# Waiting for the banks of two score tiles in front of the first of them

## What is computed

```python
q = (x @ Wq + bq).reshape(B, N, 16, 16)
k = (y @ Wk + bk).reshape(B, M, 16, 16)
v = (y @ Wv + bv).reshape(B, M, 16, 16)
scores = jnp.einsum('bnhd,bmhd->bhnm', q, k) * scale
attn = jax.nn.softmax(scores, axis=-1)
out = jnp.einsum('bhnm,bmhd->bnhd', attn, v).reshape(B, N, 256)
x = x + jnp.tanh(g_xattn[0]) * (jax.nn.relu(out @ W1 + b1) @ W2 + b2)
# then x + tanh(g_ffn[0]) * (shared expert + the top 2 of 8 routed experts)
```

## Time and profile before

| | us |
|---|---|
| median of three runs | 1035.18 |
| lowest and highest | 1034.99, 1036.46 |
| the profiled execution's own time | 1034.86 |
| its span from the first to the last instruction | 1033.1 |
| PE busy | 1011.9 (98%) |
| DVE busy | 680.7 (66%) |
| ACT busy | 612.1 (59%) |

### The profile page before, as it was taken

One profiled execution on the slowest core, in us unless ns is written; L12 is line 12 of the kernel. 1 busy time (PEld: TensorE's weight loads), 2 busy tenths in 40 slices (PEclk: granted clock), 3 DMA queues, 4 the chain that ended last, 5 costly groups with the idle time before them and its releaser, 6 DMA issues. The chain is left out here.

```text
span 1033.1 us, 15853 instructions
## 1 busy us (share of the span) xinstructions
PE 1011.9 (98%) x5821; PEld 559.6 (54%) x5821; DVE 680.7 (66%) x929; ACT 612.1 (59%) x1144; POOL 227.8 (22%) x225
## 2 busy tenths in 40 slices
PE   8899999999999999999999999998999999999998
PEld 5434445434445434544544453333666888888865
DVE  4999886896787798588788768712487322222227
ACT  3167777886677777577787767774375222222211
POOL 6129300105400103610010031020002333333310
PEclk9999999999999999999999999999999999999999
DMA  9263030430302403203033030011591111111107
GB/s 220 72 169 63 2 64 4 125 64 2 64 14 52 107 22 64 55 10 65 1 64 65 1 64 1 18 66 41 175 336 30 39 51 53 53 51 52 48 26 244
DMA packets 38282, 70.17 MB, mean 68 GB/s; under 512 B 6848, under 2 KB 23360, under 8 KB 38208
## 3 DMA queue, kind: packets, MB, share of 16 engines
q1 hardware_dynamic: 33072, 57.88, 21.6%
q0 software_dynamic: 3744, 10.23, 3.2%
q10 hardware_dynamic: 1392, 1.05, 0.4%
HBM read 33.70 MB, written 9.31 MB: 42 GB/s over the span
## 5 line engine op out<-in xcount | busy, mean ns | idle before, releaser
L770 ACT ACTIVATE probs<-ring_ps 128x512 f32<-128x512 f32 x816 | 434.0, 598 | 125.8 <-PE ring_ps L944 118.8
L1079 DVE TENSOR_REDUCE mpart<-gu_ps 128x2 f32<-128x1024 f32 x384 | 456.4, 1220 | 71.3 <-PE gu_ps L929 71.2
L944 PE MATMUL ring_ps<-qst,kst 64*128 64x512 f32 x816 | 221.8, 459 | 3.0 <-ACT probs L770 2.1
L959 PE MATMUL pv_ps<-probs,vp 128*32 128x512 f32 (+2 forms) x1664 | 222.7, 604 | 0.6 <-ACT osb L701 0.6
L944 PEld LDWEIGHTS ring_ps<-qst,kst 64*128 64x128 f32 x816 | 97.3, 180 | 205.4 <-ACT probs L770 116.2
L929 PE MATMUL gu_ps<-kst,qst 63*128 63x512 f32 (+1 forms) x1024 | 179.7, 396 | 8.7 <-DVE mpart L1079 7.5
L929 PEld LDWEIGHTS gu_ps<-kst,qst 63*128 63x128 f32 x1024 | 91.7, 185 | 64.1 <-DVE mpart L1079 40.3
L1309 ACT ACTIVATE h_sb<-gu_ps 128x512 f32<-128x512 f32 x55 | 32.8, 596 | 133.6 <-PE gu_ps L1463 133.6
L1516 DVE TENSOR_TENSOR h_sb<-h_sb,gu_ps 128x512 f32<-128x512 f32 x55 | 37.7, 686 | 112.6 <-ACT h_sb L1309 112.1
L1483 PE MATMUL y_ps<-wd,hT 128*128 x312 | 73.8, 379 | 0.0
L1300 POOL DMA_INDIRECT picked<-ysb,target x39 | 38.5, 988 | 131.5 <-DVE ysb L1557 131.5
(11 more groups left out here) (240 smaller groups left out, 1251.8 us busy)
## 6 DMA issues: line engine op xcount, KB each, us to landing
kst<-parts SPq DMA_DIRECT2D x45, 401.0 KB, 5.3
qst<-parts SPq DMA_DIRECT2D x48, 128.0 KB, 4.5
wgu<-in_WgT SPq DMA_DIRECT2D x16, 256.0 KB, 8.2
wgu<-in_WuT SPq DMA_DIRECT2D x16, 256.0 KB, 8.3
wd<-in_WdT SPq DMA_DIRECT2D x8, 512.0 KB, 9.8
wgu<-picked SPq DMA_DIRECT2D x8, 512.0 KB, 7.4
cold<-in_ctxT SPq DMA_DIRECT2D x3, 800.5 KB, 4.2
cold<-in_ctxT SPq DMA_DIRECT2D x6, 400.2 KB, 5.9
```

The source lines that it names most:

```text
L770: nc.scalar.activation(probs[0:w, m % NPB, h, :], bank_of(("st", idx))[0:w], ACT.Exp, scale=SCALE).then_inc(exp_done, 1)
L944: nc.tensor.matmul(bank_of(("st", idx))[0:w], kst[u % NKB][rows, h // 2, mt * P:mt * P + w], qst[u % NKB][rows, h // 2, :], start=True, st ...
L959: last = nc.tensor.matmul(pv_ps[32 * h:32 * h + c1 - c0, :], values[:, c0:c1], probs[0:w, m % NPB, h, :], start=(mt == 0), stop=(mt == MT ...
L1079: nc.vector.tensor_reduce(mpart[:, :, p, t, q], s_ps[:, n % NSP], AX.X, ALU.max).then_inc(s_free, 1)
```

## The change

In every step of the first 15 units, PE waits for the banks of both the third and the fourth tile before it issues the third. The waits that the two tiles have of themselves stay.

```diff
                 for pair in chunk[1:2]:
                     score(pair)
+                if u < UNITS - 1:
+                    for idx in tiles_of(m)[lead:]:
+                        free_bank(bank_owner(("st", idx)))
                 for idx in tiles_of(m)[lead:]:
                     st(idx)
```

## The result

The changed kernel takes 1040.62 us in the median of five runs (1039.77 to 1041.29), the kernel before 1035.18 (1034.94 to 1036.46). The ratio is 1.0051, with a 95% interval of 1.0038 to 1.0064: 5.4 us slower. The direction and the range of the forecast held; the size was about half of the 10.2 us that were summed.

What follows compares the result with a forecast made beforehand. A PE and ACT latency loop, 2.60 us a step, was taken as the bound. 106 steps by 0.063 + 0.033 us gave 10.2, plus 0.4, less 0.4; on 1034.86 that is 1045.1, median 0.32 higher: 1045.4 us, range 1039 to 1048.5.

Steps and rivals of the forecast that it cites:

- The bound: In the attention PE waits mostly for ACT: a loop of latencies through exponential, fourth tile, `pv` and next pair, 2.60 us.
- rival B: No difference: the wait instruction costs no more, or DVE's row maxima swallow the delay; 1035 to 1037 us, chance 0.10.
- (1) The third tile's delay: Third tile joins the fourth, 0.46 us later; its exponential starts 0.26 later; cost on the path: nothing.
- (2) The wake-up: Behind a blocking wait instruction the third tile's load comes 0.063 us later than the fourth's load did.
- Rival C: Half the price: wake-up costs 0.063 us or less and the loads start together; 1039 to 1042 us, chance 0.12.
- (3) The fourth behind the third: After a blocking wait instruction the pair's loads don't start together: 0.033 us added, the upper of bounds 0 and 0.033.
- (4) What follows the pair: `pv` loads 0.43 us after the joined pair, as after a lone fourth tile: no loss and no gain.
- (5) The count: Of 121 changed steps with the two tiles apart, 106 pay 0.096 us each, 10.2 us; the 15 others add 0.4.
- that allowance: About 9 steps with loads under 0.18 us apart, behind the row maxima's stream, counted at 0.02 us instead of 0.096.
- my 106 steps: Steps counted at full price: 121 with tiles apart, less 9 close ones and 6 with an OT job.
- Behind the attention: A delay of the attention's end is handed on whole; nothing after 712 us changes but its start.

## Why the prediction was right, and where its size was off

**The bound.** Right as to the loop. The one through the first exponential, the fourth tile, `pv` and the next pair set the step before and sets it after. Each delay of the fourth tile's load came out one for one in the period: 0.017, 0.049, 0.063 and 0.095 later gave medians of 2.620, 2.649, 2.666 and 2.694 against 2.600. Had DVE's loop been the binding one, as in rival B, these delays would have vanished in it at first; not even the smallest did, so rival B falls.

One reading on the way was wrong: that PE waits 102.1 us for exponentials. Of it, 78.0 us in 93 waits stand in front of the first tile of a step, 0.84 each, and that tile waits for PE's own stream of `pv`. Its load comes 0.99 to 1.00 behind the load of `pv` in every one of the 77 steps, in all nine kernels, and where the clock had halved the same idle time is 1.67, though the row still names an exponential:

```profile
683.92 0.50 PEld L944 LDWEIGHTS ring_ps<-qst,kst 64*128 64x128 f32 x3 [1.67 <-ACT probs L770]
```

What PE waits for exponentials in the loop is the 23.4 us, in 70 waits, in front of the fourth tile. The sum didn't use the 102.1, so nothing in it changes.

**(1) The third tile's delay** costs nothing: right, shown by the joined kernel without a wait instruction. The third exponential starts 0.23 later behind the first than before, where I had 0.26, and ACT's idle time before the first exponential fell from 0.54 to 0.36; I had said about 0.4.

**(2) The wake-up** is the term that was mis-sized. I took 0.105 - 0.042 = 0.063 from two places where the wait instruction was stopped at the first of its waits. In the change the first value is up well before the second, so that the instruction has begun when it is stopped. It then wakes in 0.059, and the term is 0.017. With the later value in both places it is 0.063, and the kernel takes 1045.37. The sentence "The changed kernel waits in this manner in every step" was the failed step: same instruction, other state. What the prediction named as a sign, 0.11 behind the exponential and a period of 2.70, came as 0.07 and 2.65. Rival C, with a chance of 0.12, is the one into whose 1039 to 1042 us the time fell. It named a wake-up of 0.063 or less, which is right, but joined it to the loads starting together, which they don't.

**(3) The fourth behind the third**: 0.033 was taken and 0.032 is there, seen twice, with and without the shorter wake-up. It is the larger part of the loss. I had chosen the upper bound because the row at 31.35 has the same form of matmul behind the same form of wait, and that held.

**(4) What follows the pair**: unchanged, 0.42 to 0.43 in every kernel.

**(5) The count.** 121 steps have the two tiles apart, and 15 of them are MX steps that swallow the change's delay; I had counted them in full. That was to be read in the trace of before: the MX job's load stood behind a wait for an exponential of its own. Of the 121, 15 have their loads under 0.18 apart, not about 9, and they lost nearly as much as the others (0.02 to 0.06 each, against 0.05), so that allowance was not needed. Compared step by step, the 77 steps without a job lost 3.5 us, 14 with SUM 0.7, 6 with XT 0.3, the remaining 9 apart from MX 0.2 and the MX steps nothing; a few steps whose tiles stood together before came out 0.3 us shorter. The sum is the 4.4 us of above. With the right term (2), my 106 steps by 0.049 would have given 5.2. The overcount stands in the forecast too: in the kernel with the later value in both places, the MX steps lost 0.5 us and not the 1.4 of 15 by 0.095, and all changed steps together 9.4. So the agreement of that kernel's time with the forecast is partly chance.

**Behind the attention** nothing was to change but its start. That holds for most of it, yet in the profiled execution the last unit, with its five banks, is 1.4 us longer. From the first tile of the last changed step to the shared expert's first weights behind the attention it is 714.14 - 670.69 = 43.45 before and 720.14 - 675.34 = 44.80 after. The last section has the cause.

## What to carry to other kernels

Of the three ways to wait measured here, the one that stands on the instruction which needs it is the cheapest; where a second wait forces a wait instruction, call the waits so that the one that comes last stays on the instruction and the early ones go into the wait instruction. Price a wait instruction in a latency loop by its state when it is stopped and by all that stands behind it, and then look at what waits next in each kind of step before multiplying. Reordering work inside a wait, as the joined pair does, neither gained nor lost here. And check the releaser that a wait's row names against the time of its event: what ends the idle time may be the engine's own earlier work.

## What the runs showed of the hardware

Prices of a wake-up on PE, from the update of the semaphore by an exponential on ACT to the start of the weight load: 0.042 us with the wait on the load, 0.059 behind a wait instruction whose first value was up, 0.105 behind one stopped at its first value, and 0.11 more for a second wait instruction. Behind a wait instruction that blocked, the second load of a pair starts 0.032 after the first, not 0.003. The Trainium skill (Perfetto Trace Analysis) says that an instruction with waits on several engines may have wait instructions inserted ahead of it. The change agrees, with 195 of them. In 188 both waits are on one and the same semaphore, so these have that effect too.

TensorE's clock fell in a place where I had not looked for it. The windows of the changed kernel and then of the one before, in the stretches that answer each other (length, busy time of PE, PEld, DVE, ACT and POOL, then the granted clock):

```profile
672.00:682.00 10.00, 7.85 (x50) 2.36 (x42) 0.41 (x2) 8.54 (x18) 0.00 (x0) 1.00 0.49 161
682.00:686.00 4.00, 3.94 (x20) 1.45 (x24) 0.08 (x1) 3.22 (x7) 0.00 (x0) 0.57 0.00 0
```

```profile
667.00:677.00 10.00, 8.68 (x51) 2.61 (x50) 0.61 (x2) 8.21 (x17) 0.00 (x0) 1.00 0.49 161
677.00:681.00 4.00, 3.64 (x26) 1.44 (x27) 1.06 (x4) 3.62 (x9) 0.00 (x0) 1.00 0.00 0
```

From about 682 us PE ran mostly at the lower of its two levels (1.2 GHz instead of 2.4), after ten microseconds in which it was busy 7.85. The eight matmuls of `pv` at 682.06 took 1.93, against 1.06 at 677.36 before. These and the matmuls behind them are the 1.4 us. It is not the change's own. The kernel with the wait between the tiles and the one with the large-job and MX steps alone, whose changed steps cost 1.6 us and nothing, had the same fall at 678 us:

```profile
678.00:682.00 4.00, 3.44 (x15) 0.85 (x15) 0.00 (x0) 3.22 (x7) 0.00 (x0) 0.58 0.00 0
...
678.00:682.00 4.00, 4.00 (x24) 1.36 (x16) 0.40 (x2) 3.15 (x7) 0.00 (x0) 0.57 0.00 0
```

The others had none in this stage. The stretch that takes 43.45 us before and 44.80 in the changed kernel takes 44.64 and 44.79 in these two and 43.45 to 43.62 in the five others. How busy PE was just ahead doesn't tell them apart: from 668 to 678 us it was busy 8.79 in the kernel with the wait between the tiles, which had the fall, and 7.91 in the one with the swapped order, which had none. What brings it on stays open.

It comes and goes between executions of one kernel, as far as their mean clocks tell: six of the 38 runs of the kernel before that were taken beside the experiments have 0.997 and took 1035.88 to 1036.93 us, the five with 1.000 took 1035.08 to 1035.31, and the 27 between scatter from 1034.45 to 1036.58. Of the changed kernel, the three runs at 0.997 took 1040.62 to 1041.29, and the two at 1.000 took 1039.77 and 1040.01. At 1.000 the two kernels are thus 4.7 us apart, close to the 4.4 of the changed steps. That three of five changed runs were at 0.997 may be chance; whether the change makes the fall more frequent stays open.
